# A causal-attention and LoRA layer on one core: the negated row maxima by a copy and a subtraction, and GpSimd's division one pair earlier

## The chip, the cores and the metric

The kernel runs on one core of a Trainium2 chip. The metric is the device time of one launch in microseconds (us), lower is better.

## The reference

One layer over x of shape (2, 2048, 512), float32: attention with a residual, then a feed-forward part with a residual.

```python
x = x + attn(layernorm(x), Wq, Wk, Wv, Wo)      # 16 heads of 32, rotary positions, causal
x = x + ffn(layernorm(x), base_w, base_b, router_w, router_b, lora_A, lora_B)

# attn, for each batch and head
scores = q @ k.T / sqrt(32); scores = where(causal, scores, -inf)
ctx = softmax(scores) @ v                        # then ctx @ Wo.T
# ffn: x @ base_w.T + base_b, plus 2.0 * the two best of 8 rank-16 experts
```

## The kernel before

Three stages follow one another: `project` (queries, keys and values into scratch tensors in HBM), `attend` and `finish` (output projection and feed-forward part). The change is in `attend`.

`attend` works on 8 groups, each of 4 heads of one batch entry. A group's queries are 4 tiles of 512 rows, called units, t = 0 to 3. A unit has 4(t + 1) steps, one for each block of 128 keys, 40 steps a group, and two steps make a pair: 20 pairs a group. The last pairs of the four units are 1, 5, 11 and 19.

In each step TensorE computes transposed scores of the 4 heads (`scores`, L665), ScalarE takes their exponential (L749) into a ring of 4 steps, GpSimd zeroes the later keys of a diagonal step (L605) and adds the two steps of a pair, two heads at a time (L620), and TensorE multiplies by the values (L679) and sums the pair over the keys with ones (L695, L699). GpSimd's order is `add_pairs`: for each pair the selections where they are needed, two additions of 1,024 elements a partition or fewer, and at two pairs after a unit's end the division `divide` (L630).

The exponential is of score minus row maximum. The maximum has to be there before the unit's first step, so TensorE computes the scores a second time, the other way round, in 80 items a group (`item`, L653), half a group ahead: an item is two heads by 128 queries by up to 512 keys, in one of two PSUM buffers, and item k waits until item k-2 is reduced. VectorE reduces each item (`item_max`: L769, or L775 with the causal mask for the diagonal chunk) into `part`. When the last item of a unit is reduced, `unit_max` (L781 to L797) reduces `part` over the chunks to 16 numbers a partition (4 heads by 4 blocks of queries), negates them, splits them into a part rounded to the format that the matmul reads (`F32R`) and the rest, and transposes both into `neg_rows`. SyncE's queue writes these as two more rows of the queries' stack (`shift_rows`), which two rows of ones in the keys' stack add to the scores.

The units' ends of `unit_max` fall in fixed pairs of a group: unit 2 in pair 1, unit 3 in pair 9, and unit 0 and 1 of the next group in pairs 11 and 15. The first group starts with the items of units 0 and 1 ahead of everything.

After a unit's end VectorE transposes its sums (L803), inverts them behind the next item (L807) and transposes them back behind the one after (`turn_back`, L812); GpSimd multiplies them into the unit's output (L630), which waits for L812 and for ScalarE's copy of the output; SyncE's `store` then sends it to HBM. All engines follow an order fixed in the program; VectorE's is, for each pair, the transpose of the sums if a unit ended with the pair before, then the pair's items, then `unit_max` if one is due.

Of the kernel before, what the change touches and what calls it, by code (L numbers as in the profile page):

```python
# [26 lines left out]
F32R = mybir.dt.float32r  # L27
BF16 = mybir.dt.bfloat16
ALU = mybir.AluOpType
ACT = mybir.ActivationFunctionType  # L30
AX = mybir.AxisListType

P = 128
# [7 lines left out]
SUB = TT // P  # L41
HG = 4
# [62 lines left out]
def unit_ended_before(p, pairs):  # L105

    e = p - pairs
    return [(int(e < 0), t) for t in range(QT) if LAST_PAIR[t] == e % NPAIR]


def wait_alone(eng, semaphore, value, passed):

    eng.wait_ge(semaphore, value)
    eng.sem_inc(passed, 1)
# [332 lines left out]
def attend(nc, qk_scr, v_scr, ctx_scr, shared, early):  # L447
    with ExitStack() as ctx:
        def sb(name, shape, dt=F32):
            return ctx.enter_context(nc.sbuf_tensor(name, shape, dt))  # L450

        def sem(name):
            return ctx.enter_context(nc.semaphore(name))
# [11 lines left out]
        ones = sb("a_ones", [P, DK])  # L465
        mask = sb("a_mask", [P, TT])
        part = sb("a_part", [P, HG * SUB, QT])
        max_both = sb("a_max_both", [P, 2, HG * SUB])
        neg_parts = sb("a_neg_parts", [P, 2, HG, SUB])
        neg_rows = sb("a_neg_rows", [P, 2, 32])  # L470
        st_ps = ctx.enter_context(nc.psum_tensor("a_st", [P, BANKS, TT], F32))
# [13 lines left out]
        av_copied, sum_turned = sem("a_av_copied"), sem("a_sum_turned")  # L485
        item_done, max_done = sem("a_item_done"), sem("a_max_done")
        dve_passed, pool_passed = sem("a_dve_passed"), sem("a_pool_passed")
        reduced = sem("a_reduced")
        rsum_done, rsum_turned, out_done = sem("a_rsum_done"), sem("a_rsum_turned"), sem("a_out_done")
        neg_done, rows_done = sem("a_neg_done"), sem("a_rows_done")  # L490
        ctx_stored = [sem("a_ctx_stored0"), sem("a_ctx_stored1")]
# [6 lines left out]
        def exps(g, s, h):  # L498

            return HG * NSTEP * g + HG * s + h + 1 + BANKS  # L500

        def diagonal_steps(g, s):

            t, j = STEPS[s]
            return SUB * QT * g + SUB * t + (j - t * SUB) + 1

        def pairs(g, p):

            return NPAIR * g + p + 1 + FREE
# [74 lines left out]
        @block.gpsimd  # L584
        def _(pool):
            for semaphore in (av_copied, sum_turned, out_done, rows_done, *shift_loaded, *ctx_stored):
                pool.sem_inc(semaphore, START)

            pool.memset(mask[:, :], 0.0).then_inc(zeroed, 1)
            pool.wait_ge(zeroed, 1)  # L590
            pool.affine_select(mask[:, TT - P:TT], mask[:, TT - P:TT], pattern=[[-1, P]], compare_op=ALU.is_ge,
                               fill=MASKED, base=0, channel_multiplier=1).then_inc(consts_done, 1)
            pool.wait_ge(consts_done, 1)
            for n in range(2):
                pool.memset(k_stack[n][96:98].bitcast(F32), 1.0).then_inc(key_ones, 1)
                pool.wait_ge(key_ones, n + 1)


            def drop_later_keys(g, s):

                t, j = STEPS[s]
                q0 = (j - t * SUB) * P
                block = probs[:, s % RING, :, q0:q0 + P]
                wait_alone(pool, exp_done, exps(g, s, HG - 1), pool_passed)
                pool.affine_select(block, block, pattern=[[0, HG], [1, P]], compare_op=ALU.is_ge, fill=0.0, base=0,  # L605
                                   channel_multiplier=-1).then_inc(masked, 1)

            def add_pairs(g, first):
                for p in range(NPAIR):
                    s = 2 * p  # L610
                    t, j = STEPS[s]
                    q0 = max(0, j + 1 - t * SUB) * P
                    if j >= t * SUB:
                        drop_later_keys(g, s)
                        drop_later_keys(g, s + 1)
                        pool.wait_ge(masked, diagonal_steps(g, s + 1))
                    pool.wait_ge(pair_done, pairs(g, p - 2))
                    for h in range(0, HG, 2):
                        pool.wait_ge(exp_done, exps(g, s + 1, h + 1))
                        pool.tensor_tensor(pair[:, p % 2, h:h + 2, q0:TT], probs[:, s % RING, h:h + 2, q0:TT],  # L620
                                           probs[:, (s + 1) % RING, h:h + 2, q0:TT], ALU.add).then_inc(pair_added, 1)
                    for before, t_out in unit_ended_before(p, 2):
                        if not (before and first):
                            divide(g - before, t_out)

            def divide(g, t):

                pool.wait_ge(rsum_turned, 4 * g + t + 1)
                pool.wait_ge(av_copied, 4 * g + t + 1 + START)
                pool.tensor_tensor(ctx_st[:, t % 2], ctx_st[:, t % 2], rsum_b[:, :], ALU.mult).then_inc(out_done, 1)  # L630

            add_pairs(0, True)
            with pool.Fori(1, GROUPS) as g:
                add_pairs(g, False)
            divide(GROUPS - 1, QT - 1)
# [126 lines left out]
        def _(dve):  # L762
# [18 lines left out]
            def unit_max(g, t, items):  # L781

                U = 4 * g + t
                dve.wait_ge(max_done, items + 2)
                found = part[:, :, 0:t + 1]
                dve.tensor_reduce(max_both[:, 0], found, AX.X, ALU.max, negate=True).then_inc(reduced, 1)
                dve.tensor_reduce(max_both[:, 1].bitcast(F32R), found, AX.X, ALU.max).then_inc(reduced, 1)
                dve.wait_ge(rows_done, U + START)
                dve.tensor_reduce(neg_parts[:, 0].rearrange("p h q -> p (h q)").bitcast(F32R), found, AX.X, ALU.max,
                                  negate=True).then_inc(neg_done, 1)  # L790
                dve.wait_ge(reduced, 2 * U + 2)
                with nc.allow_low_precision(reason="one exact difference, rounded as it is written"):
                    dve.tensor_reduce(neg_parts[:, 1].rearrange("p h q -> p (h q)").bitcast(F32R),
                                      max_both[:, :, :].rearrange("p n m -> p m n"), AX.X, ALU.add).then_inc(neg_done, 1)
                dve.wait_ge(neg_done, 2 * U + 2)
                dve.wait_ge(shift_loaded[t % 2], SHIFTS * (2 * g + t // 2) + START)
                dve.transpose(neg_rows[:, t % 2, :], neg_parts[:, :, :, :].rearrange("p n h q -> p (n h q)")).then_inc(rows_done, 1)  # L797

# [16 lines left out]
            def group(g, first, last):  # L815
                for p in range(NPAIR):
                    items = [(n, k) for n, k in items_of_pair(p, first) if not (n and last)]
                    ended = [(g - before, t) for before, t in unit_ended_before(p, 1) if not (before and first)]
                    for unit in ended:
                        turn_sums(*unit)  # L820
                    for i, (n, k) in enumerate(items):
                        item_max(g + n, k)
                        for unit in ended:
                            if i == 0:
                                invert(*unit)
                            if i == 1:
                                turn_back(*unit)
                    if len(items) < 2:
                        for unit in ended:
                            if not items:  # L830
                                invert(*unit)
                            turn_back(*unit)
                    for n, t in units_ended_at_pair(p, first):
                        if not (n and last):
                            issued = items_before(p + 1, first)
                            unit_max(g + n, t, NITEM * g + (min(issued, NITEM) if last else issued))
# [451 lines left out]
def layer(nc, x, wq_t, wk_t, wv_t, wo_t, rope, base_t, base_b, router_t, router_b, lora_a, lora_b, out):  # L1288

    qk_scr = nc.dram_tensor("qk_scratch", [4, GROUPS, P, SEQ], F32, kind="Internal").ap()  # L1290
    v_scr = nc.dram_tensor("v_scratch", [GROUPS, SEQ, P], F32, kind="Internal").ap()
    ctx_scr = nc.dram_tensor("ctx_scratch", [GROUPS, P, SEQ], F32, kind="Internal").ap()
    with ExitStack() as ctx:

        shared = ctx.enter_context(nc.sbuf_tensor("shared", [P, W_RING * DM], F32))[:, :]
        early = Early(nc, ctx, shared, ctx_scr, wo_t)
        project(nc, x, wq_t, wk_t, wv_t, rope, qk_scr, v_scr, shared)
        attend(nc, qk_scr, v_scr, ctx_scr, shared, early.loads)
        finish(nc, early, x, wo_t, base_t, base_b, router_t, router_b, lora_a, lora_b, out)
# [43 lines left out]
```

## Time and profile before

| | |
|---|---|
| median of 3 runs | 1798.36 us (1798.25 to 1802.1) |
| the profiled execution, its own time | 1798.25 us |
| its span, first to last instruction | 1796.3 us |
| TensorE (PE) busy | 1667.7 us, 93% |
| VectorE (DVE) busy | 1130.8 us, 63% |
| ScalarE (ACT) busy | 823.7 us, 46% |
| GpSimd (POOL) busy | 882.0 us, 49% |
| mean granted TensorE clock | 0.968 |
| the attention stage | from about 317 to 1489 us of the span |

The share of busy time is a mean over stages with different limits. A matmul's end is modelled, so a busy PE isn't a PE at its peak. Idle time of an engine costs something only where another comes to wait for it.

### The profile page before, as it was taken

What the parts mean: (1) busy time and instruction counts of PE and PEld (TensorE: products, weight loads), DVE (VectorE), ACT (ScalarE), POOL (GpSimd) and SP (SyncE); (2) the same over time, 40 slices, a digit from 0 to 9 for tenths busy, and PEclk for the clock granted to TensorE, in tenths of its full rate; (3) what the DMA queues carried; (4) which work ended last, traced back from release to release, by engine and by line L of the source; (5) the groups of instructions that cost most, each with busy time, mean ns of one, the idle gap of its engine ahead of it and who ended that gap; (6) DMA issues with size and microseconds to landing.
All of it is one profiled execution on the core that took longest, in us unless ns stands there. A gap on an engine that the chain in (4) does not pass through costs nothing. (4 is left out here: it accounts for less than half of the span.)

```text
span 1796.3 us, 30755 instructions
## 1 busy us (share of the span) xinstructions
PE 1667.7 (93%) x9440; PEld 989.6 (55%) x9440; DVE 1130.8 (63%) x2278; ACT 823.7 (46%) x1544; POOL 882.0 (49%) x558
## 2 busy tenths in 40 slices
PE   6999997599999999989999999999999985999998
PEld 5888885244454454444444444445445423777776
DVE  6667663567676676667667766767767405555664
ACT  3222221045665665646556655656656663222321
POOL 1332333346666666756667666666666672111111
PEclk9999999579999999999999999999999997999999
DMA  5556545751142133134115106107102003222321
GB/s 176 205 184 233 191 158 186 165 112 30 25 97 70 26 85 81 25 71 96 25 34 127 31 19 142 25 7 159 25 7 78 7 6 118 73 92 70 102 85 47
DMA packets 103185, 156.90 MB, mean 87 GB/s; under 512 B 10544, under 2 KB 43824, under 8 KB 100400
## 3 DMA queue, kind: packets, MB, share of 16 engines
q1 hardware_dynamic: 93296, 136.10, 28.1%
q10 hardware_dynamic: 9792, 19.40, 2.9%
q8 instruction: 74, 1.21, 0.3%
q14 instruction: 23, 0.19, 0.0%
HBM read 96.23 MB, written 58.72 MB: 86 GB/s over the span
## 5 line engine op out<-in xcount | busy, mean ns | idle before, releaser
L749 ACT ACTIVATE a_probs<-a_st 128x512 f32<-128x512 f32 (+3 forms) x1280 | 648.4, 532 | 459.3 <-PE a_st L665 416.9
L620 POOL TENSOR_TENSOR a_pair<-a_probs 128x1024 f32<-128x1024 f32 (+2 forms) x320 | 613.9, 1938 | 267.9 <-ACT a_probs L749 254.4
L769 DVE TENSOR_REDUCE a_part<-a_mx 128x2 f32<-128x1024 f32 x384 | 460.9, 1219 | 226.8 <-PE a_mx L653 226.0
L665 PE MATMUL a_st<-a_q_stack,a_k_stack 98*128 98x512 f32 (+3 forms) x1280 | 523.8, 421 | 30.2 <-ACT a_probs L749 20.6
L665 PEld LDWEIGHTS a_st<-a_q_stack,a_k_stack 98*128 98x128 f32 x1280 | 240.9, 189 | 389.2 <-ACT a_probs L749 250.0
L653 PE MATMUL a_mx<-a_k_stack,a_q_stack 96*128 96x512 f32 (+3 forms) x1280 | 380.9, 384 | 50.3 <-DMA a_q_stack<-qk_scratch 24.5
L775 DVE CUSTOM_DVE_ANT_0 a_mx<-a_mx,a_mask 128x384 f32<-128x384 f32 (+3 forms) x512 | 239.5, 515 | 100.1 <-PE a_mx L653 99.3
L653 PEld LDWEIGHTS a_mx<-a_k_stack,a_q_stack 96*128 96x128 f32 x1280 | 235.2, 197 | 106.2 <-DVE a_part L769 40.3
L211 POOL TENSOR_TENSOR p_rot<-p_mul 128x1024 f32<-128x1024 f32 x32 | 90.8, 2838 | 213.3 <-DVE p_mul L406 213.3
L605 POOL TENSOR_SCALAR_AFFINE_SELECT a_probs<-a_probs 128x512 f32<-128x512 f32 x128 | 80.9, 634 | 154.4 <-ACT a_probs L749 154.2
L985 POOL TENSOR_TENSOR f_x<-f_x,f_bias 128x512 f32<-128x512 f32 x32 | 41.3, 1324 | 230.4 <-DVE f_xn L1178 230.4
L679 PE MATMUL a_av<-a_probs,shared 128*32 128x512 f32 (+3 forms) x1280 | 151.5, 546 | 0.0
L679 PE MATMUL a_av<-a_probs,a_v 128*32 128x512 f32 (+3 forms) x1280 | 151.5, 546 | 0.0
L699 PE MATMUL a_sum<-a_pair,a_ones 128*32 128x512 f32 (+2 forms) x1280 | 140.0, 509 | 0.3 <-POOL a_pair L620 0.3
L405 DVE TENSOR_TENSOR p_mul<-p_pair,p_tab 128x1024 f32<-128x1024 f32 x32 | 39.1, 1222 | 64.4 <-PE p_pair L275 64.4
L324 ACT ACTIVATE p_rot_hi<-p_rot 128x1024 fp32r<-128x1024 f32 x32 | 34.0, 1062 | 89.3 <-POOL p_rot L211 89.3
L275 PE MATMUL p_pair<-p_xt_hi,p_w_hi 128*128 128x512 f32 x256 | 72.6, 406 | 1.6 <-DVE p_xt_lo L396 1.6
L699 PEld LDWEIGHTS a_sum<-a_pair,a_ones 128*32 128x32 f32 x1280 | 40.3, 110 | 58.1 <-issue 57.5
L775 DVE DVE_READ_ACCUMULATOR2_ANT a_part<- 128x1 f32 x512 | 72.1, 141 | 0.0
L410 DVE TENSOR_TENSOR p_rot_lo<-p_rot,p_rot_hi 128x1024 fp32r<-128x1024 f32 x32 | 50.8, 1588 | 33.1 <-ACT p_rot_hi L324 33.1
L275 PE MATMUL p_pair<-p_xt_hi,p_w_lo 128*128 128x512 f32 x256 | 70.9, 399 | 0.0
L275 PE MATMUL p_pair<-p_xt_lo,p_w_hi 128*128 128x512 f32 x256 | 70.9, 399 | 0.0
(134 smaller groups left out, 1586.4 us busy)
## 6 DMA issues: line engine op xcount, KB each, us to landing
a_q_stack<-qk_scratch SPq DMA_DIRECT2D x96, 256.0 KB, 5.1
a_k_stack<-qk_scratch SPq DMA_DIRECT2D x21, 1024.0 KB, 12.8
qk_scratch<-p_rot_hi SPq DMA_DIRECT2D x32, 512.0 KB, 3.1
qk_scratch<-p_rot_lo SPq DMA_DIRECT2D x32, 512.0 KB, 3.9
v_scratch<-p_v_st SPq DMA_DIRECT2D x32, 256.0 KB, 6.1
ctx_scratch<-a_ctx_st SPq DMA_DIRECT2D x32, 256.0 KB, 2.6
f_ctx<-ctx_scratch SPq DMA_DIRECT2D x8, 1024.0 KB, 8.8
f_x<-in_x SPq DMA_DIRECT2D x8, 1024.0 KB, 8.0
```

What stands on the lines that cost most here:

```text
L211: pool.tensor_tensor(rot[:, par], mul[:, par, :, 0, :], mul[:, par, :, 1, :], ALU.add).then_inc(rot_done, 1)
L275: mm = pe.matmul(pair_ps[p % 2][:, half, :], w[:, kt, cols], a[:, u, kt, :], start=(n == 0), stop=(n == len(passes) - 1))
L410: dve.tensor_tensor(rot_lo[:, p % 2], rot[:, p % 2], rot_hi[:, p % 2].bitcast(F32), ALU.subtract).then_inc(rot_lo_done, 1)
L605: pool.affine_select(block, block, pattern=[[0, HG], [1, P]], compare_op=ALU.is_ge, fill=0.0, base=0, channel_multiplier=-1).then_inc(mask ...
L620: pool.tensor_tensor(pair[:, p % 2, h:h + 2, q0:TT], probs[:, s % RING, h:h + 2, q0:TT], probs[:, (s + 1) % RING, h:h + 2, q0:TT], ALU.add ...
L653: mm = pe.matmul(mx_ps[k % 2][:, n, 0:width], q_stack[0:96, t, h, qi * P:(qi + 1) * P], k_stack[par][0:96, h, c * TT:c * TT + width], star ...
L665: pe.matmul(st_ps[:, n % BANKS, q0:TT], k_stack[par][0:98, h, j * P:(j + 1) * P], q_stack[0:98, t, h, q0:TT], start=True, stop=True).then_ ...
L679: mm = pe.matmul(av_ps[h * DK:(h + 1) * DK, q0:TT], vb[par][:, j, h * DK:(h + 1) * DK], probs[:, s % RING, h, q0:TT], start=j == 0, stop=s ...
L699: mm = pe.matmul(sum_ps[h * DK:(h + 1) * DK, q1:TT], ones[:, :], pair[:, p % 2, h, q1:TT], start=unit_first and q1 == q0, stop=unit_last, ...
L749: act.activation(probs[:, s % RING, h, q0:TT], st_ps[:, (HG * s + h) % BANKS, q0:TT], ACT.Exp, scale=SCORE_SCALE).then_inc(exp_done, 1)
L769: dve.tensor_reduce(heads_part[:, 2 * hp:2 * hp + 2, qi, c], mx_ps[k % 2][:, :, :], AX.X, ALU.max).then_inc(max_done, 1)
L775: ins = dve.tensor_tensor_reduce(out=mx_ps[k % 2][:, n, 0:width], in0=mx_ps[k % 2][:, n, 0:width], in1=mask[:, TT - width:TT], scale=1.0, ...
```

## The change

In `unit_max` the 16 maxima are taken and negated once, into `neg_max`; a copy rounds them into the first half of `neg_parts`, and a subtraction writes the rest into the second half. Before, four reductions made the same two halves: one negated and one rounded into `max_both`, one negated and rounded into `neg_parts`, and a sum over the pair in `max_both`. In `add_pairs` the division of a finished unit stands one pair after its end, not two. SyncE's `store` keeps its place, two pairs after.

```diff
-        max_both = sb("a_max_both", [P, 2, HG * SUB])
+        neg_max = sb("a_neg_max", [P, HG * SUB])
...
-        reduced = sem("a_reduced")
+        reduced, rounded = sem("a_reduced"), sem("a_rounded")
...
-                    for before, t_out in unit_ended_before(p, 2):
+                    for before, t_out in unit_ended_before(p, 1):
                         if not (before and first):
                             divide(g - before, t_out)
...
                 dve.wait_ge(max_done, items + 2)
-                found = part[:, :, 0:t + 1]
-                dve.tensor_reduce(max_both[:, 0], found, AX.X, ALU.max, negate=True).then_inc(reduced, 1)
-                dve.tensor_reduce(max_both[:, 1].bitcast(F32R), found, AX.X, ALU.max).then_inc(reduced, 1)
+                dve.tensor_reduce(neg_max[:, :], part[:, :, 0:t + 1], AX.X, ALU.max, negate=True).then_inc(reduced, 1)
+                dve.wait_ge(reduced, U + 1)
                 dve.wait_ge(rows_done, U + START)
-                dve.tensor_reduce(neg_parts[:, 0].rearrange("p h q -> p (h q)").bitcast(F32R), found, AX.X, ALU.max,
-                                  negate=True).then_inc(neg_done, 1)
-                dve.wait_ge(reduced, 2 * U + 2)
-                with nc.allow_low_precision(reason="one exact difference, rounded as it is written"):
-                    dve.tensor_reduce(neg_parts[:, 1].rearrange("p h q -> p (h q)").bitcast(F32R),
-                                      max_both[:, :, :].rearrange("p n m -> p m n"), AX.X, ALU.add).then_inc(neg_done, 1)
-                dve.wait_ge(neg_done, 2 * U + 2)
+                neg = neg_max[:, :].rearrange("p (h q) -> p h q", q=SUB)
+                dve.tensor_copy(neg_parts[:, 0].bitcast(F32R), neg).then_inc(rounded, 1)
+                dve.wait_ge(rounded, U + 1)
+                dve.tensor_tensor(neg_parts[:, 1].bitcast(F32R), neg, neg_parts[:, 0], ALU.subtract).then_inc(neg_done, 1)
+                dve.wait_ge(neg_done, U + 1)
```

## Rows read from the trace of the kernel before

**Rows 1.** Busy us by engine (instructions) in the steady attention stretch, clock, DMA.
```profile
core 0: us, PE busy (x) PEld busy (x) DVE busy (x) ACT busy (x) POOL busy (x), PEclk, DMA share, GB/s
400.00:1427.00 1027.00, 991.20 (x6350) 494.21 (x6349) 708.61 (x1527) 610.99 (x1203) 671.54 (x440) 1.00 0.25 56
```

**Rows 2.** Waits of PE, 400 to 1427 us: total us, times, longest.
```profile
PE a_mx L653 <- DVE a_part L769: 13.6, 34, 0.7
```

**Rows 3.** Timeline at unit 2's end: start, us, engine, line, operation, [idle before].
```profile
943.77 1.22 POOL L605 TENSOR_SCALAR_AFFINE_SELECT a_probs<-a_probs 128x512 f32<-128x512 f32 x2
...
947.61 0.64 PE L679 MATMUL a_av<-a_probs,shared 128*32 128x256 f32 x8
...
950.11 4.72 POOL L620 TENSOR_TENSOR a_pair<-a_probs 128x1024 f32<-128x1024 f32 x2 [2.19 <-ACT a_probs L749]
...
950.46 0.20 DVE L786 TENSOR_REDUCE a_max_both<-a_part 128x16 f32<-128x48 f32 x1
...
951.15 0.21 DVE L797 STREAM_TRANSPOSE a_neg_rows<-a_neg_parts 128x32 f32<-128x32 f32 x1 [0.15 <-DVE a_neg_parts L793]
...
953.62 1.17 DVE L769 TENSOR_REDUCE a_part<-a_mx 128x2 f32<-128x1024 f32 x1
...
954.70 0.70 DVE L812 STREAM_TRANSPOSE a_rsum_b<-a_rsum 128x512 f32<-128x512 f32 x1
...
955.43 0.62 PE L653 MATMUL a_mx<-a_k_stack,a_q_stack 96*128 96x512 f32 x2
...
956.33 4.71 POOL L620 TENSOR_TENSOR a_pair<-a_probs 128x1024 f32<-128x1024 f32 x2 [1.50 <-ACT a_probs L749]
```

**Rows 4.** Timeline of the projection stage: VectorE's subtraction and GpSimd's addition.
```profile
145.49 2.39 POOL L211 TENSOR_TENSOR p_rot<-p_mul 128x1024 f32<-128x1024 f32 x1 [0.80 <-DVE p_mul L406]
...
145.93 3.04 DVE L410 TENSOR_TENSOR p_rot_lo<-p_rot,p_rot_hi 128x1024 fp32r<-128x1024 f32 x1 [0.60 <-ACT p_rot_hi L324]
...
154.48 1.21 DVE L410 TENSOR_TENSOR p_rot_lo<-p_rot,p_rot_hi 128x1024 fp32r<-128x1024 f32 x1
...
154.72 3.23 POOL L211 TENSOR_TENSOR p_rot<-p_mul 128x1024 f32<-128x1024 f32 x1 [6.84 <-DVE p_mul L406]
```

**Rows 5.** Timeline of the last stage: two of GpSimd's four successive additions, one subtraction.
```profile
1518.58 1.26 POOL L985 TENSOR_TENSOR f_x<-f_x,f_bias 128x512 f32<-128x512 f32 x1
...
1519.34 1.06 DVE L140 TENSOR_TENSOR f_base_lo<-shared,f_base_hi 128x512 fp32r<-128x512 f32 x1
...
1519.81 1.72 POOL L985 TENSOR_TENSOR f_x<-f_x,f_bias 128x512 f32<-128x512 f32 x1
```

**Rows 6.** Groups by line and form: busy us, mean ns of one, idle before.
```profile
L1222 DVE COPY f_gate_x<-f_h 128x512 f32<-128x512 f32 x8 | 3.4, 427 | 0.3
```

**Rows 7.** Timeline at unit 0's end.
```profile
1018.55 4.70 POOL L620 TENSOR_TENSOR a_pair<-a_probs 128x1024 f32<-128x1024 f32 x2 [3.61 <-ACT a_probs L749]
...
1019.54 0.21 DVE L797 STREAM_TRANSPOSE a_neg_rows<-a_neg_parts 128x32 f32<-128x32 f32 x1 [0.16 <-DVE a_neg_parts L793]
...
1021.25 1.20 DVE L769 TENSOR_REDUCE a_part<-a_mx 128x2 f32<-128x1024 f32 x1
...
1023.66 0.63 PE L653 MATMUL a_mx<-a_k_stack,a_q_stack 96*128 96x512 f32 x2
```

**Rows 8.** Timeline at unit 1's end.
```profile
910.45 4.72 POOL L620 TENSOR_TENSOR a_pair<-a_probs 128x1024 f32<-128x1024 f32 x2 [3.65 <-ACT a_probs L749]
...
913.72 2.36 DVE L769 TENSOR_REDUCE a_part<-a_mx 128x2 f32<-128x1024 f32 x2 [1.53 <-PE a_mx L653]
...
915.00 0.44 PE L653 MATMUL a_mx<-a_k_stack,a_q_stack 96*128 96x128 f32 x2 [0.40 <-DVE a_part L769]
```

**Rows 9.** Timeline at unit 3's end.
```profile
1007.06 0.64 POOL L605 TENSOR_SCALAR_AFFINE_SELECT a_probs<-a_probs 128x512 f32<-128x512 f32 x1 [2.03 <-ACT a_probs L749]
...
1008.96 0.43 DVE L775 CUSTOM_DVE_ANT_0 a_mx<-a_mx,a_mask 128x256 f32<-128x256 f32 x1 [1.58 <-PE a_mx L653]
```

**Rows 10.** Timeline of PE near the kernel's end.
```profile
1780.60 0.69 PE L1054 MATMUL f_out_ps<-f_b_hi,f_mt_hi 128*128 128x512 f32 x1 [2.17 <-DVE f_mt_lo L1231]
```

**Rows 11.** Busy us by engine and clock (the third number from the end) behind it.
```profile
1780.60:1786.00 5.40, 5.40 (x17) 4.23 (x18) 1.38 (x2) 0.00 (x0) 0.00 (x0) 0.68 0.00 2
```

## Prediction

> **What bounds the kernel now.** The change lies in the attention stage, so I read the busy time by stretch first. In [rows 1] TensorE is busy for 991.2 of 1027 us, at its full clock, while VectorE has 709 and GpSimd 672. Whatever holds TensorE back here is paid in full, and a delay on VectorE or GpSimd is paid only where TensorE comes to wait for it. The list of waits, second, says how near that is: TensorE already waits for the running maxima of VectorE, 34 times in this stretch and never over 0.7 us [rows 2]. The two `a_mx` buffers give VectorE little room: item k may be multiplied only when item k-2 has been reduced. Third I read the timeline around each place that the change touches, for how much room is left there.
>
> **What VectorE does at a unit's end, before.** The chain is three reductions that don't depend on each other, a fourth that does, and the transpose. In [rows 3] it runs from 950.46 to 951.36 (951.15 + 0.21), 0.90 us, for the unit t = 2. GpSimd's pair addition runs all that time (950.11 to 954.83, two instructions of about 2.36) and the chain isn't slowed by it.
>
> **What it does after.** One reduction, a copy that needs it, a subtraction that needs both, the transpose. Three dependent steps instead of two. A step behind two waits starts 0.16 us after its predecessor's end, as the transpose does [rows 3], so with about 0.2 us for each small instruction the free-running chain takes 0.2 + 0.16 + 0.2 + 0.03 to 0.16 + 0.2 + 0.16 + 0.21, about 1.1 to 1.3 us: 0.2 to 0.4 longer than before, times 32 units. If that were all it would cost nearly nothing, since VectorE is idle for 1.5 us after most of these places; only in the first 30 us, where TensorE waits on VectorE item by item, would 0.3 us show.
>
> **The term that decides: GpSimd.** The projection stage shows what an instruction of VectorE with two inputs in SBUF does beside a GpSimd addition. Alone, the subtraction of line 410 takes 1.21 us; started at 145.93 inside an addition that ends at 147.88, it takes 3.04, that is, it ends 1.09 us after the addition [rows 4]. It was held for all the rest of it. The other way round, an addition started at 154.72 inside such a subtraction takes 3.23 instead of 2.39. So the two exclude one another for whole instructions. The last stage shows who comes next when additions stand back to back: GpSimd's second, 1518.58 to 1519.84, holds the subtraction of 1519.34 (1.06 us); then the subtraction goes, and it is the third addition, nominally begun at 1519.81, that is stretched to 1.72 us [rows 5]. VectorE slips in between two additions.
> The reductions of before, and the maxima in PSUM with the mask, show none of this beside GpSimd (the chain of [rows 3] runs inside an addition). The new subtraction has two SBUF inputs, `neg_max` and `neg_parts[:, 0]`. The new copy has one; no row shows such a copy beside GpSimd. One row bears on it: a copy of 512 elements in SBUF takes 427 ns [rows 6], while the subtraction of 1024 takes 1.21 us, so the copy moves more than one element in a cycle, and I take it to use the same second path. Bounds: it is never held (0), or held to the end of the addition under way. I take the upper one.
> The Trainium skill (SBUF — State Buffer, Who interferes with whom) says that reductions never contend with GpSimd, that a copy does when it runs in the two-port mode, and that a `tensor_tensor` with both inputs in SBUF contends with GpSimd's reads, the later one being blocked wholly. By that rule the sum is the one below; without its sentence on copies it would be the smaller one of the first rival.
>
> **Priced place by place.** Each unit's chain falls at a fixed place in the loop of 20 pairs, four places in a group.
> Unit t = 2 [rows 3]. The copy is due at 950.46 + 0.19 + 0.16 = 950.81, the first addition ends at 952.47; the copy goes then, till 952.6. The second addition follows and holds the subtraction till 954.95; that is done at 955.1, the transpose runs from 955.25 to 955.46, 4.1 us late. Behind it VectorE has the transpose of the sums and an item, and begins the next item, k = 50, 2.10 us later (951.36 to 953.62, less 0.16 of waiting): 957.56, done 1.17 later at 958.73. TensorE's item k = 52 needs that; it began at 955.43 and now begins at 958.78. Loss 3.35 us.
> Unit t = 0 [rows 7]. The additions run from 1018.55 to 1023.25. By the same steps the transpose ends at 1023.86 instead of 1019.75. The item of 1021.25 began 1.50 after that end, so it now runs from 1025.36 to 1026.56, and TensorE's item of 1023.66 begins at 1026.61. Loss 2.95 us.
> Unit t = 1 [rows 8]. Additions till 915.17, the transpose ends at 915.86. VectorE's item of 913.72 begins at 915.95 and ends at 917.1, and TensorE's item that now starts at 915.00, already 0.40 late, starts at 917.15. Loss 2.15 us.
> Unit t = 3 [rows 9]. Only a selection of 0.64 us is near (1007.06), and VectorE's next item is 1.58 us of idle away. At worst 0.64 + 0.4 later: nothing lost.
> The places repeat with the same offsets in all groups: seven each for the first three, since the first group is filled from a head start. Sum 7 x (3.35 + 2.95 + 2.15) = 59.2. The first group's own t = 2, beside a shorter addition, and the start: about 1.5, an estimate. Together 61 us.
>
> **The clock.** TensorE would now stand still for 2 to 2.7 us at 21 places. Before the end of the kernel it stood for 2.17 us and then ran at 0.68 of its clock over 5.4 us, that is partly at the lower of its two levels, 1.2 GHz: 1.7 us lost [rows 10, 11]. Bounds for 21 places: 0 and 36 us. I put in 5, a seventh, as most gaps have work close on both sides.
>
> **The earlier division.** GpSimd's division (1.28 us) goes from behind the second pair after a unit's end to behind the first. Costs and gains: after unit 3 it stands ahead of the selections of 943.77, which end at 946.3 instead of 945.0, and TensorE wants the first at 947.61: hidden, 1.9 us to spare for the selection it needs first. After unit 0, it waits for the transposed reciprocals (954.70 + 0.70) after the additions' end at 954.83, and the next addition begins 0.35 later than 956.33, with 3 us in hand before its sums. Even with VectorE 4 us late, the division ends at 960.7, where that next addition could begin at 959.7 and is wanted at 968. Nothing frees a buffer that anyone waits for: the store stays where it is in SP's queue. 0 us, with bounds of -0.5 and +1 a group. SP's other issues, the shift rows among them, are due several pairs before they are used.
>
> **Sum.** Span 1796.3 + 61 + 5 = 1862; its own time is 1.95 us above the span (1798.25), which is the median of the runs to 0.1. 1864 us.
>
> **Rivals.**
> - *One hold instead of two* (the copy isn't held). The subtraction alone, due at 951.0, waits till 952.45; the transpose ends at 952.96, 1.6 late; TensorE loses 1.0 at t = 2 and 0.5 at t = 0, nothing at t = 1. 7 x 1.5 + 1 = 11 us: 1810. For it: no row shows a held copy. Against: [rows 6].
> - *No hold for so small an instruction*, the other side. Instructions of 16 elements might pass between GpSimd's accesses; the held ones of [rows 4, 5] have 512 and 1024. Then three small instructions replace four, the chain is about as long, and the time is 1798 to 1800, no change. It decides if a copy or subtraction in a running addition takes under 0.3 us. The skill (VectorE: DVE Perf Modes, Rules for kernel authors) advises to minimise the count of chained instructions, which by itself would make this part a gain, at most 32 x 0.1 us on an engine with time to spare.
> - *The clock falls nearly each time*: 61 + 36, 1895. For it: [rows 10, 11]. Against: 2.17 us is the shortest gap that I found a fall behind, and most of the new ones would be about that or broken up by short work.
> - *Faster*: the division's move removes a wait that the trace doesn't name. Nothing speaks for it; 2 us at best.
>
> **Chances.** Two holds 0.66; one hold 0.13; no hold 0.12; two holds and the low clock 0.05; faster 0.04. The two-hold case alone spans 1845 to 1885 (the places' sum off by a quarter, clock 0 to 15). To leave out no more than two in ten the range must reach the one-hold case: 1806 to 1890. A measurement here can tell about 0.2%, 3.6 us, from no change: faster 0.04, same 0.12, slower 0.84.
>
> **What would show it.** In the changed trace the copy or the subtraction of a unit's end should last 1.5 to 2.4 us at three of four places and under 0.3 at the fourth; the transpose should end about 4 us after the reduction; TensorE's waits for `a_part` should grow from 0.7 to 2 to 3 us, three in each group, and each group should be 8 to 9 us longer. Divisions should begin one pair earlier with no wait of TensorE behind them. Small instructions at 0.2 us beside additions prove the prediction wrong; so does a group of unchanged length.

## The result, and the profile after

The change makes the kernel slower: 1892.78 us median of 4 runs (1881.79 to 1897.07) against 1798.68 us (1798.25 to 1802.1, 4 runs), a ratio of 1.051 with a 95% interval of 1.0462 to 1.0556. That is 94 us more, 29 us above the forecast of 1864 and 3 us above the top of the range. The profiled execution took 1886.59 us, its span is 1884.6 us, 88.3 us longer than before, and its mean granted clock is 0.945, before 0.968.

The chain first. The rows of its three last instructions give the least, median and longest duration in ns, then the first and last start in us:

```profile
L789 DVE CAST a_neg_parts<-a_neg_max x32: 174/1218/1929, 337.4 to 1513.5; 128x16 fp32r<-128x16 f32 x32
L791 DVE TENSOR_TENSOR a_neg_parts<-a_neg_max,a_neg_parts x32: 174/2291/2320, 337.6 to 1513.7; 128x16 fp32r<-128x16 f32 x32
L794 DVE STREAM_TRANSPOSE a_neg_rows<-a_neg_parts x32: 211/211/214, 337.8 to 1514.2; 128x32 f32<-128x32 f32 x32
```

The copy (shown as CAST) and the subtraction move 16 elements a partition and take 174 ns when nothing is in the way; half of the copies take 1.2 us or more, half of the subtractions 2.3 us or more. The timeline at a unit 2's end shows why; it answers to [rows 3]:

```profile
995.02 4.71 POOL L620 TENSOR_TENSOR a_pair<-a_probs 128x1024 f32<-128x1024 f32 x2 [2.18 <-ACT a_probs L749]
995.37 0.20 DVE L785 TENSOR_REDUCE a_neg_max<-a_part 128x16 f32<-128x48 f32 x1
...
995.70 1.73 DVE L789 CAST a_neg_parts<-a_neg_max 128x16 fp32r<-128x16 f32 x1
...
997.47 2.30 DVE L791 TENSOR_TENSOR a_neg_parts<-a_neg_max,a_neg_parts 128x16 fp32r<-128x16 f32 x1
...
999.94 0.21 DVE L794 STREAM_TRANSPOSE a_neg_rows<-a_neg_parts 128x32 f32<-128x32 f32 x1 [0.17 <-DVE a_neg_parts L791]
...
1001.94 0.44 PE L653 MATMUL a_mx<-a_k_stack,a_q_stack 96*128 96x128 f32 x2 [1.90 <-DVE a_part L769]
...
1003.18 1.22 PE L653 MATMUL a_mx<-a_k_stack,a_q_stack 96*128 96x512 f32 x2 [0.52 <-DVE a_part L769]
...
1003.90 1.28 POOL L630 TENSOR_TENSOR a_ctx_st<-a_ctx_st,a_rsum_b 128x512 f32<-128x512 f32 x1 [4.16 <-DVE a_rsum_b L809]
```

GpSimd's two additions run from 995.02 to 999.73, the first to about 997.4. The copy ends at 997.43, with the first; the subtraction, which needs the copy, gets no room between the two and ends at 999.77, with the second. From the start of the reduction to the end of the transpose it is 4.78 us, before 0.90. TensorE, which waited 0.7 us at most in [rows 2], now waits 1.90 and then 0.52 us.

At a unit 0's end the same holds stand (copy 1.74, subtraction 2.29), and the wait ends with VectorE's L775:

```profile
1075.50 0.44 PE L653 MATMUL a_mx<-a_k_stack,a_q_stack 96*128 96x128 f32 x2 [1.50 <-DVE a_part L775]
...
1076.69 0.73 PE L653 MATMUL a_mx<-a_k_stack,a_q_stack 96*128 96x512 f32 x2 [0.46 <-DVE a_part L769]
```

At a unit 3's end no addition is under way, and the chain runs free, 1.11 us from 1057.10 to 1058.21:

```profile
1057.10 0.22 DVE L785 TENSOR_REDUCE a_neg_max<-a_part 128x16 f32<-128x64 f32 x1
1057.45 0.17 DVE L789 CAST a_neg_parts<-a_neg_max 128x16 fp32r<-128x16 f32 x1
1057.66 0.17 DVE L791 TENSOR_TENSOR a_neg_parts<-a_neg_max,a_neg_parts 128x16 fp32r<-128x16 f32 x1
1058.00 0.21 DVE L794 STREAM_TRANSPOSE a_neg_rows<-a_neg_parts 128x32 f32<-128x32 f32 x1 [0.17 <-DVE a_neg_parts L791]
```

TensorE's waits for the maxima over the whole span (total us, times, longest). Before, these two rows had 21.2 us in 47 times and 4.1 us in 12:

```profile
PE a_mx L653 <- DVE a_part L769: 53.6, 68, 2.2
...
PE a_mx L653 <- DVE a_part L775: 13.8, 18, 1.5
```

That is 42 us more waiting, less than half of the 88. The rest is in the clock, as the experiments with repeated matmuls will show. The stretch that answers to [rows 1], and five stretches of 2 us behind the wait of unit 2 above (the granted clock is the third number from the end):

```profile
400.00:1513.00 1113.00, 1035.44 (x6321) 507.07 (x6324) 774.99 (x1489) 612.03 (x1200) 668.77 (x437) 0.95 0.23 52
1000.00:1002.00 2.00, 0.10 (x2) 0.06 (x1) 2.00 (x5) 0.60 (x1) 0.00 (x0) 1.00 1.11 226
1002.00:1004.00 2.00, 1.48 (x5) 1.07 (x6) 2.00 (x6) 0.60 (x1) 0.10 (x1) 0.74 1.22 298
1004.00:1006.00 2.00, 2.00 (x7) 0.64 (x10) 1.45 (x3) 1.09 (x2) 2.00 (x2) 0.50 1.08 209
1006.00:1008.00 2.00, 2.00 (x16) 0.40 (x8) 0.00 (x0) 0.00 (x0) 2.00 (x2) 0.50 1.06 232
1008.00:1010.00 2.00, 2.00 (x7) 1.02 (x4) 0.00 (x0) 0.41 (x1) 1.81 (x1) 0.56 0.66 218
```

Full speed while TensorE waits, then half of it, the 1.2 GHz level, for some 7 us, nearly six of them without a gap in TensorE's work. The mean of [rows 1] was 1.00, and 0.95 is the mean here. By the trace's record of the granted clock it falls behind 19 of the 21 late places (seven each at the ends of units 2, 0 and 1), and stays low for 3.4 to 10.2 us each time, 102 us in all.

Both kernels issue the same 9,440 matmuls in the same order, so one can be laid on the other. In the steady part the lag grows at three places of each group alone, those of units 2, 0 and 1, and not at unit 3's. Over the seven units 2 it grows by 34.0 us, over the seven units 0 by 29.3, over the seven units 1 by 28.2, 91.5 in all; 3 us are won back elsewhere, over 2 of them in the first group, where the low clock at the stage's start ends at 371.5 us and not at 377.9. It does so in some runs and not in others: with the division alone it ended at 370.8, with the chain alone at 378.2.

### The profile page after: what moved, and what is told of

It reads as the page before. It is cut to its first block and busy times, and to the rows that moved or that the text cites. A ratio compares the mean times of both kernels' runs of the same rounds, so it can differ in the third digit from the quotient of the medians.

```text
span 1884.6 us, 30755 instructions
## 1 busy us (share of the span) xinstructions
PE 1713.1 (91%) x9440; PEld 1001.3 (53%) x9440; DVE 1201.0 (64%) x2246; ACT 826.3 (44%) x1544; POOL 881.6 (47%) x558
## 5 line engine op out<-in xcount | busy, mean ns | idle before, releaser
L769 DVE TENSOR_REDUCE a_part<-a_mx 128x2 f32<-128x1024 f32 x384 | 460.9, 1218 | 234.2 <-PE a_mx L653 233.2
L665 PE MATMUL a_st<-a_q_stack,a_k_stack 98*128 98x512 f32 (+3 forms) x1280 | 531.1, 429 | 29.7 <-ACT a_probs L749 20.3
L653 PE MATMUL a_mx<-a_k_stack,a_q_stack 96*128 96x512 f32 (+3 forms) x1280 | 392.3, 393 | 93.1 <-DVE a_part L769 53.6
L665 PEld LDWEIGHTS a_st<-a_q_stack,a_k_stack 98*128 98x128 f32 x1280 | 247.2, 194 | 395.0 <-ACT a_probs L749 239.8
L775 DVE CUSTOM_DVE_ANT_0 a_mx<-a_mx,a_mask 128x384 f32<-128x384 f32 (+3 forms) x512 | 239.0, 513 | 108.3 <-PE a_mx L653 108.3
L679 PE MATMUL a_av<-a_probs,shared 128*32 128x512 f32 (+3 forms) x1280 | 161.7, 579 | 0.0
L679 PE MATMUL a_av<-a_probs,a_v 128*32 128x512 f32 (+3 forms) x1280 | 157.1, 565 | 0.0
L699 PE MATMUL a_sum<-a_pair,a_ones 128*32 128x512 f32 (+2 forms) x1280 | 148.7, 538 | 0.3 <-POOL a_pair L620 0.3
L630 POOL TENSOR_TENSOR a_ctx_st<-a_ctx_st,a_rsum_b 128x512 f32<-128x512 f32 x32 | 40.9, 1279 | 69.2 <-DVE a_rsum_b L809 69.2
L775 DVE DVE_READ_ACCUMULATOR2_ANT a_part<- 128x1 f32 x512 | 72.2, 141 | 0.0
```

The source lines that it names most:

```text
L653: mm = pe.matmul(mx_ps[k % 2][:, n, 0:width], q_stack[0:96, t, h, qi * P:(qi + 1) * P], k_stack[par][0:96, h, c * TT:c * TT + width], star ...
L665: pe.matmul(st_ps[:, n % BANKS, q0:TT], k_stack[par][0:98, h, j * P:(j + 1) * P], q_stack[0:98, t, h, q0:TT], start=True, stop=True).then_ ...
L679: mm = pe.matmul(av_ps[h * DK:(h + 1) * DK, q0:TT], vb[par][:, j, h * DK:(h + 1) * DK], probs[:, s % RING, h, q0:TT], start=j == 0, stop=s ...
L699: mm = pe.matmul(sum_ps[h * DK:(h + 1) * DK, q1:TT], ones[:, :], pair[:, p % 2, h, q1:TT], start=unit_first and q1 == q0, stop=unit_last, ...
L769: dve.tensor_reduce(heads_part[:, 2 * hp:2 * hp + 2, qi, c], mx_ps[k % 2][:, :, :], AX.X, ALU.max).then_inc(max_done, 1)
L775: ins = dve.tensor_tensor_reduce(out=mx_ps[k % 2][:, n, 0:width], in0=mx_ps[k % 2][:, n, 0:width], in1=mask[:, TT - width:TT], scale=1.0, ...
```

## The experiments

**The division alone.**

```diff
-                    for before, t_out in unit_ended_before(p, 2):
+                    for before, t_out in unit_ended_before(p, 1):
```

> The kernel before with the division alone moved one pair ahead. Theory (the chain does all the harm): GpSimd's selections and additions behind the division move by at most 1.3 us and TensorE never waits for them, so 1798 to 1800 us, ratio 0.999 to 1.002. Rival (the division does part of the harm, since GpSimd then waits for VectorE ahead of its next additions): some us a group, 1810 or more.

Measured: 1798.3 us (1796.35 to 1804.73, 12 runs), ratio 0.9988 (0.9974 to 1.0002). In the timeline the division now stands ahead of the next pair's additions, which begin 1.98 us after the last ones' end instead of 1.50, and nobody comes to wait for them:

```profile
949.16 2.38 POOL L620 TENSOR_TENSOR a_pair<-a_probs 128x1024 f32<-128x1024 f32 x1
952.28 1.29 POOL L630 TENSOR_TENSOR a_ctx_st<-a_ctx_st,a_rsum_b 128x512 f32<-128x512 f32 x1 [0.74 <-DVE a_rsum_b L812]
953.52 4.71 POOL L620 TENSOR_TENSOR a_pair<-a_probs 128x1024 f32<-128x1024 f32 x2
```

The division costs nothing, as forecast.

**The chain alone**: the changed kernel with the division back behind the second pair.

```diff
-                    for before, t_out in unit_ended_before(p, 1):
+                    for before, t_out in unit_ended_before(p, 2):
```

> The changed chain, with the division back at two pairs. Theory: the copy lasts 1.2 to 1.8 us and the subtraction 2.3 us at three of four places as in the changed kernel, time 1880 to 1897 us. Rival (division): clearly below the changed kernel, by the 10 us or more that the moved division adds when VectorE is late.

Measured: 1894.19 us (1891.17 to 1895.73, 4 runs), ratio 1.0513 (1.0487 to 1.054), TensorE's wait on L769 53.2 us in 67 times, clock 0.941. The whole loss is the chain's.

**Only the subtraction.** The rounded half comes from a second reduction, as it did before, and the subtraction stays. The chain then has one instruction that GpSimd could hold.

```diff
                 dve.tensor_reduce(neg_max[:, :], part[:, :, 0:t + 1], AX.X, ALU.max, negate=True).then_inc(reduced, 1)
-                dve.wait_ge(reduced, U + 1)
                 dve.wait_ge(rows_done, U + START)
-                dve.tensor_copy(neg_parts[:, 0].bitcast(F32R), neg).then_inc(rounded, 1)
+                dve.tensor_reduce(neg_parts[:, 0].rearrange("p h q -> p (h q)").bitcast(F32R), part[:, :, 0:t + 1],
+                                  AX.X, ALU.max, negate=True).then_inc(rounded, 1)
+                dve.wait_ge(reduced, U + 1)
                 dve.wait_ge(rounded, U + 1)
```

> The changed chain, but the rounded half comes from a second reduction and not from the copy; the subtraction with two SBUF inputs stays, the division is at two pairs. Theory (each of the two is held for what is left of the addition under way): one hold of 1.4 to 1.9 us for the subtraction, the transpose ends 1.6 us later than before, TensorE loses 1.0 us at the end of unit 2, 0.5 at unit 0 and nothing at unit 1, and gaps this short leave the clock up: 1806 to 1815 us. Rival (a hold lasts to the end of both additions, whichever instruction asks): the subtraction lasts over 4 us and the time stays at 1880 or more.

Measured: 1801.62 us (1799.66 to 1804.58, 10 runs), ratio 1.001 (0.9996 to 1.0023). The timeline at a unit 2's end:

```profile
947.99 4.71 POOL L620 TENSOR_TENSOR a_pair<-a_probs 128x1024 f32<-128x1024 f32 x2 [2.19 <-ACT a_probs L749]
948.34 0.20 DVE L785 TENSOR_REDUCE a_neg_max<-a_part 128x16 f32<-128x48 f32 x1
...
948.46 0.20 DVE L788 TENSOR_REDUCE a_neg_parts<-a_part 128x16 fp32r<-128x48 f32 x1
...
948.69 1.72 DVE L792 TENSOR_TENSOR a_neg_parts<-a_neg_max,a_neg_parts 128x16 fp32r<-128x16 f32 x1
...
950.57 0.21 DVE L795 STREAM_TRANSPOSE a_neg_rows<-a_neg_parts 128x32 f32<-128x32 f32 x1 [0.17 <-DVE a_neg_parts L792]
```

Both reductions pass inside the addition in 0.20 us each, and the subtraction is held to the end of the first one. The hold is as forecast. Its price isn't: the transpose is 1.54 us late (2.44 from the reduction's start, before 0.90), and TensorE loses 0.3 us at unit 2 and nothing at unit 0, where the expectation had 1.0 and 0.5; the time lies below its 1806 to 1815 us, and can't be told from no change.

**Only the copy.** Before's chain, with the third reduction replaced by a copy of the first one's output.

```diff
-                dve.tensor_reduce(neg_parts[:, 0].rearrange("p h q -> p (h q)").bitcast(F32R), found, AX.X, ALU.max,
-                                  negate=True).then_inc(neg_done, 1)
                 dve.wait_ge(reduced, 2 * U + 2)
+                dve.wait_ge(rows_done, U + START)
+                dve.tensor_copy(neg_parts[:, 0].bitcast(F32R),
+                                max_both[:, 0].rearrange("p (h q) -> p h q", q=SUB)).then_inc(neg_done, 1)
```

> The chain of before, but the rounded half is copied from the unrounded one and not reduced again; no subtraction. Theory (a copy of 16 elements takes GpSimd's path too): the copy lasts 1.4 to 1.9 us beside an addition, the sum behind it 0.2 us, time 1806 to 1815 us. Rival (the copy is slow only because it is the instruction ahead of a held subtraction): under 0.3 us and 1799 us.

Measured: 1804.14 us (1801.88 to 1810.08, 10 runs), ratio 1.0027 (1.0012 to 1.0043). The copy and the reduction behind it, in ns:

```profile
L790 DVE CAST a_neg_parts<-a_max_both x32: 174/1123/1831, 336.6 to 1428.2; 128x16 fp32r<-128x16 f32 x32
L793 DVE TENSOR_REDUCE a_neg_parts<-a_max_both x32: 172/174/181, 336.7 to 1428.7; 128x16 fp32r<-128x32 f32 x32
```

A copy of 16 elements is held too, to 1.83 us; a reduction of 32 never is. At a unit 2's end the transpose is 1.62 us late and TensorE loses 0.4 us, at a unit 0's 0.1; the time is again below the 1806 to 1815 us expected. By their ratios the two edits apart cost 2 and 5 us (0.001 and 0.0027 of 1798, the first with an interval that holds 1); summed over the places in the traces it is 2.1 and 3.6 us. Together they cost 94.

**The waits filled.** In the changed kernel the scores' matmul just ahead of each of the 21 late items, and of the same item in the first group, where nothing is late, is issued six more times, with the same operands and output, so that TensorE works where it waited. It tells the clock's share from the waiting itself.

```diff
-            def scores(g, par, s, h):
+            def scores(g, par, s, h, extra=0):
...
-                pe.matmul(st_ps[:, n % BANKS, q0:TT], k_stack[par][0:98, h, j * P:(j + 1) * P],
-                          q_stack[0:98, t, h, q0:TT], start=True, stop=True).then_inc(st_done, 1)
+                for _ in range(extra + 1):
+                    mm = pe.matmul(st_ps[:, n % BANKS, q0:TT], k_stack[par][0:98, h, j * P:(j + 1) * P],
+                                   q_stack[0:98, t, h, q0:TT], start=True, stop=True)
+                mm.then_inc(st_done, 1)
...
+                            extra = 6 if i < len(due) and due[i] == late else 0
```

> The changed kernel, with one scores matmul repeated six more times (about 0.2 us each, same result, written over itself) right ahead of each of the 21 items for which TensorE waits longest: the gap is mostly filled with work that nobody needs. Theory (some 49 us of the loss are waits, some 40 the lower clock behind them): the waits' ends don't move, the granted clock stays at 1.0 there, and the time falls to 1845 to 1865 us although TensorE does more. Rival (all of the loss is waiting, the clock's fall costs nothing since VectorE sets the pace): 1882 to 1897 us as without the repeats, or more.

Measured: 1853.92 us (1849.44 to 1856.65, 4 runs), ratio 1.0303 (1.0266 to 1.034). With 132 more matmuls (22 places) it is 39 us faster than the changed kernel. Holds, waits and clock:

```profile
L793 DVE CAST a_neg_parts<-a_neg_max x32: 174/1221/1929, 336.9 to 1478.4; 128x16 fp32r<-128x16 f32 x32
L795 DVE TENSOR_TENSOR a_neg_parts<-a_neg_max,a_neg_parts x32: 174/2290/2325, 337.1 to 1478.6; 128x16 fp32r<-128x16 f32 x32
```

```profile
PE a_mx L653 <- DVE a_part L773: 34.3, 67, 1.3
```

```profile
400.00:1478.00 1078.00, 1029.15 (x6451) 516.86 (x6455) 773.09 (x1490) 611.77 (x1199) 669.20 (x437) 0.99 0.23 54
```

VectorE is held exactly as in the changed kernel and the items are late as there; TensorE's idle time is shorter, and the clock no longer falls at the ends of units 0 and 1. At those of unit 2 it still falls, six times of seven, for 3.4 us, though the waits ahead are only two of 0.51 us:

```profile
983.92 0.73 PE L653 MATMUL a_mx<-a_k_stack,a_q_stack 96*128 96x512 f32 x2 [0.52 <-DVE a_part L773]
```

```profile
986.00:988.00 2.00, 2.00 (x12) 0.22 (x4) 0.05 (x1) 0.01 (x1) 2.00 (x1) 0.50 1.01 207
```

The mean of 0.99 hides these six, and the expectation, a clock of 1.0 at all the places, missed them. Laid over the kernel before, a unit 0 now costs 2.2 us and a unit 1 1.8, which is about their items' lateness (2.36 and 1.76 us in the changed kernel); a unit 2 costs 4.3 us with the fall and 2.5 in the one case without. So the 39 us are what the prevented and shortened falls had cost, and not all of the clock's share. By the two ratios it is 1.051 - 1.0303, 37 us of 1798, and with both intervals (0.0047 and 0.0037, together 0.006) about 37 ± 11.

**The same repeats in the kernel before.** The edit is that of the last experiment, made to the kernel before.

> The same repeats in the kernel before, where there are no such gaps. Both theories: 21 x 6 x 0.22 = 27 us more TensorE work with nothing to hide it, 1820 to 1828 us. It gives the price of the repeats by themselves; under 1805 would mean that TensorE isn't the bound at these places.

Measured: 1821.0 us (1820.07 to 1828.81, 4 runs), ratio 1.0118 (1.0087 to 1.0149). By themselves the repeats cost 23 us, about 132 times 0.17, so they aren't a gain of their own: what they win in the changed kernel they win by standing in its waits.

**Shorter additions.** In the changed kernel GpSimd adds one head at a time, four instructions a pair instead of two.

```diff
-                    for h in range(0, HG, 2):
-                        pool.wait_ge(exp_done, exps(g, s + 1, h + 1))
-                        pool.tensor_tensor(pair[:, p % 2, h:h + 2, q0:TT], probs[:, s % RING, h:h + 2, q0:TT],
-                                           probs[:, (s + 1) % RING, h:h + 2, q0:TT], ALU.add).then_inc(pair_added, 1)
+                    for h in range(HG):
+                        pool.wait_ge(exp_done, exps(g, s + 1, h))
+                        pool.tensor_tensor(pair[:, p % 2, h, q0:TT], probs[:, s % RING, h, q0:TT],
+                                           probs[:, (s + 1) % RING, h, q0:TT], ALU.add).then_inc(pair_added, 1)
...
-                pe.wait_ge(pair_added, 2 * (NPAIR * g + p) + 2)
+                pe.wait_ge(pair_added, 4 * (NPAIR * g + p) + 4)
```

> The changed kernel, with GpSimd's additions in four instructions of one head (about 1.28 us) and not two of two heads (2.37 us). Theory (a hold lasts for the rest of one GpSimd instruction): the copy lasts 0.6 to 0.9 us, the subtraction 1.3 us, the transpose ends some 1.7 us later than before and not 3.9, TensorE's loss is 0.5 to 1.2 us a place and the clock mostly stays up: 1808 to 1825 us. Rival (holds last until GpSimd has no work): as long as in the changed kernel, 1880 us or more.

Measured: 1813.74 us (1808.74 to 1815.57, 6 runs), ratio 1.0074 (1.0048 to 1.01). The timeline at a unit 2's end:

```profile
952.96 5.00 POOL L620 TENSOR_TENSOR a_pair<-a_probs 128x512 f32<-128x512 f32 x4 [0.90 <-ACT a_probs L749]
...
954.02 0.20 DVE L785 TENSOR_REDUCE a_neg_max<-a_part 128x16 f32<-128x48 f32 x1
...
954.36 1.15 DVE L789 CAST a_neg_parts<-a_neg_max 128x16 fp32r<-128x16 f32 x1
...
955.54 1.21 DVE L791 TENSOR_TENSOR a_neg_parts<-a_neg_max,a_neg_parts 128x16 fp32r<-128x16 f32 x1
...
956.92 0.21 DVE L794 STREAM_TRANSPOSE a_neg_rows<-a_neg_parts 128x32 f32<-128x32 f32 x1 [0.17 <-DVE a_neg_parts L791]
```

An addition now takes 1.25 us, and each small instruction is held for at most one of these (the copy for longer than the 0.6 to 0.9 us expected). The hold follows the length of GpSimd's instruction, and with it 79 of the 94 us are gone: the transpose is 2.21 us late instead of 3.88, TensorE loses 1.0 us at unit 2, 0.5 at unit 0 and 0.1 at unit 1, and the clock stays up at these places (mean 0.966). It falls once where before it didn't, behind two waits of 0.45 us for ScalarE near the stage's end, and 4.2 us are lost there.

**Later additions.** In the changed kernel both additions wait for all four exponentials of the pair's second step, which moves their start behind most of the chain.

```diff
-                        pool.wait_ge(exp_done, exps(g, s + 1, h + 1))
+                        pool.wait_ge(exp_done, exps(g, s + 1, HG - 1))
```

> The changed kernel with both chains as they are; GpSimd's first addition of a pair waits for the exponentials of all four heads of the second step and not of two, which starts it some 1.25 us later. Theory (the loss hangs on an addition being under way when VectorE comes to the copy): at the ends of units 2 and 0 copy and subtraction are through before the addition starts and take 0.2 us each; at unit 1 the copy is through and the subtraction is held for one addition, 2.2 us, worth 1 us to TensorE; the clock stays up. 1800 to 1812 us, over 80 us less than the changed kernel, by a wait more. Rival (the small instructions are slow by themselves or by their dependence): 1885 us or more.

Measured: 1806.95 us (1804.12 to 1825.56, 11 runs), ratio 1.005 (1.0027 to 1.0073). The same three instructions, and their timeline at a unit 2's end:

```profile
L789 DVE CAST a_neg_parts<-a_neg_max x32: 174/175/177, 337.0 to 1432.7; 128x16 fp32r<-128x16 f32 x32
L791 DVE TENSOR_TENSOR a_neg_parts<-a_neg_max,a_neg_parts x32: 174/175/2374, 337.2 to 1432.9; 128x16 fp32r<-128x16 f32 x32
```

```profile
953.87 0.18 DVE L789 CAST a_neg_parts<-a_neg_max 128x16 fp32r<-128x16 f32 x1
...
954.08 0.17 DVE L791 TENSOR_TENSOR a_neg_parts<-a_neg_max,a_neg_parts 128x16 fp32r<-128x16 f32 x1
...
954.38 4.74 POOL L620 TENSOR_TENSOR a_pair<-a_probs 128x1024 f32<-128x1024 f32 x2 [3.37 <-ACT a_probs L749]
```

The chain is word for word that of the changed kernel, and without an addition beside it it costs next to nothing. Only unit 1's subtraction still meets one (up to 2.37 us); it costs 0.7 us a group. So the loss comes from the meeting of the two engines and not from the chain's length.

None of these beats the kernel before: the nearest is the division alone, whose interval holds 1.

## Why the prediction missed its number

The direction, the two holds and the places were right. The step that failed is the size of one term, the clock: "Bounds for 21 places: 0 and 36 us. I put in 5, a seventh". It measured about 43 us. The other large term, the waits, was 12 us too large, so the total missed by less than the clock alone did; that is luck.

| term | predicted | measured |
|---|---|---|
| free chain, from its reduction's start | 1.1 to 1.3 us | 1.11 us |
| copy and subtraction at unit 2 | 1.8 and 2.35 us | 1.73 and 2.30 us |
| transpose late at unit 2 | 4.1 us | 3.88 us |
| TensorE's late item at unit 2 / 0 / 1 | 3.35 / 2.95 / 2.15 us | 2.84 / 2.36 / 1.76 us |
| unit 3 | 0 | 0 |
| lateness of the items in all | 61 us | 49 us |
| clock | 5 us | about 43 us |
| division | 0 | 0 |

*The two holds.* Confirmed, for both instructions, by the copy-only and the subtraction-only kernels, which hold each by itself, and by the two edits on GpSimd, which shorten or remove the holds with the chain unchanged. The Trainium skill (SBUF — State Buffer, Who interferes with whom) says that the engine that issues first keeps the shared ports for its whole instruction, and that reductions don't take part; the trace agrees, with 1.73 and 2.30 us for two instructions that take 0.17 alone, and 0.17 to 0.20 for the reductions beside the same additions. The Trainium skill (VectorE: DVE Perf Modes, Rules for kernel authors) advises to minimise the count of chained instructions. The runs don't bear that out here: three in place of four cost 94 us.

*The waits.* At unit 2 the late item begins 7.81 us after the reduction (995.37 to 1003.18), before 4.97, so 2.84 later; at unit 0 2.36, at unit 1 1.76. Seven times their sum is 48.7 us, 12 less than forecast; 1.5 of the 12 are the first group's, whose chains run free. For the rest, the reason shows when the runs are put side by side at unit 2: one hold makes the transpose 1.54 and 1.62 us late and costs 0.3 and 0.4, short additions 2.21 and 1.0, two holds 3.88 and 2.84. Each time it is the lateness less 1.0 to 1.3 us. The prediction's step ("done 1.17 later ... TensorE's item k = 52 needs that") left a cover of only 0.75 (4.1 less 3.35), since it kept the spacing of before, 2.10 us from the transpose's end to the next but one item of VectorE; it is 1.81 here (1000.15 to 1001.96), as VectorE, once late, finds its items ready. The rest of the 0.51 us at unit 2 is the transpose, 3.88 us late and not 4.1. The cover is also why the one-hold rival was priced too high, 1.5 us a group where 0.3 to 0.5 were lost at TensorE: one hold nearly fits into the cover, and two are far beyond it. So 2 and 5 us apart become 94 together.

*The clock.* By the laid-over traces the late places cost 91.5 us, of which 48.7 are the items' lateness; the other 43 lie in the microseconds behind them, where the same matmuls take longer, and the windows show 0.50. The seven ends of unit 1 show the price with the wait nearly constant (2.05 to 2.16 us): they cost 1.8 us twice, where the clock stayed up, 3.3 once, where it was low for 3.4 us, 4.5 twice for 6.8 us, and 6.2 twice for 10.2 us. The filled kernel takes 37 ± 11 us away by experiment and leaves six falls at some 1.7 us each; with these it is 47 ± 11, which agrees.

The forecast's reason, "most gaps have work close on both sides", is refuted: [rows 10, 11] already had a fall behind 2.17 us, and here falls stand behind 1.90 and 0.52 us with 0.7 us of work between. The trace of the kernel before had more against it, in the very stretch of [rows 1] that the prediction read as "at its full clock". Its mean of 1.00 is rounded and hides two falls, of 6.8 and 3.4 us, behind stops of TensorE in the middle of dense work ("issue": it waited for nothing that the profile shows):

```profile
799.78 0.57 PE L665 MATMUL a_st<-a_q_stack,a_k_stack 98*128 98x256 f32 x1 [3.07 <-issue]
1080.34 0.38 PE L665 MATMUL a_st<-a_q_stack,a_k_stack 98*128 98x256 f32 x1 [3.28 <-issue]
```

```profile
800.00:802.00 2.00, 2.00 (x6) 1.69 (x7) 0.76 (x1) 0.77 (x2) 1.06 (x1) 0.50 1.05 213
1081.00:1084.00 3.00, 3.00 (x14) 1.41 (x13) 2.69 (x7) 1.18 (x4) 1.00 (x2) 0.50 0.99 202
```

The upper bound, 36, was itself too low, since 21 places cost 2.0 us on average and not 1.7. The rival "the clock falls nearly each time" had 1895 and a chance of 0.05; it was the case that came true (19 of 21). That its number is only 2 us off is luck in part, as its waits were 12 us too large and its clock about 7 too small. The term deserved at least the middle of its bounds: 61 + 18 would have been 1877.

The changed kernel's runs spread by 15 us, and the clock with them: the run of 1881.79 us had a mean of 0.947, that of 1897.07 us 0.939. The profiled one, with 0.945, is among the quicker; that is why its span grew by 88 us and the median by 94.

*What stays open.* When the clock falls and when not. At unit 1's end TensorE waited 2.16 us each time, and once the clock stayed up, once it fell. The rows of TensorE and the windows behind them, first without, then with the fall:

```profile
959.90 0.44 PE L653 MATMUL a_mx<-a_k_stack,a_q_stack 96*128 96x128 f32 x2 [2.16 <-DVE a_part L769]
```

```profile
805.10 0.69 PE L653 MATMUL a_mx<-a_k_stack,a_q_stack 96*128 96x128 f32 x2 [2.16 <-DVE a_part L769]
```

```profile
960.00:961.00 1.00, 1.00 (x7) 0.46 (x11) 1.00 (x2) 0.34 (x1) 0.00 (x0) 1.00 0.05 8
...
807.00:809.00 2.00, 2.00 (x10) 0.79 (x3) 0.00 (x0) 0.05 (x1) 0.00 (x0) 0.50 0.01 2
```

The first place cost 1.8 us in all, the second 4.5. Matmuls of the same forms surround both, and in the kernel with the waits filled the clock fell behind waits of 0.51 us, so the length of the wait alone doesn't decide; what does was not tried.

## What to carry to other kernels

Before an instruction is put in for another on VectorE, ask what GpSimd is doing at that moment, and not how many elements it has: a small copy or subtraction in SBUF can cost a whole GpSimd instruction, a reduction doesn't, and two dependent ones beside successive additions cost two. A hold costs next to nothing while it fits into the slack that the pacing engine leaves (some 1.0 to 1.3 us here), and what goes beyond it is paid, so price the sum of the delays at one place, not each edit by itself. Where TensorE sets the pace, a repeated wait of about 2 us should be priced with its clock: here that nearly doubled it, and moving or cutting the other engine's work won back 79 to 86 of the 94 us.

## What was unexpected of the hardware

TensorE's clock went to its lower level after waits of 1.4 to 2.2 us between stretches of dense work, at 19 of 21 places, and stayed there for 3.4 to 10.2 us (0.74, 0.50, 0.50, 0.56 in windows of 2 us at the one shown), at a price of about 2 us a place. With six repeated matmuls in each wait it stayed up at 15 of the 21, and at the other six it fell behind two waits of 0.51 us. Waits of the same 2.16 us ended differently. And a copy of only 16 elements a partition, 0.17 us by itself, is held for what is left of GpSimd's instruction: 1.73 us beside additions of 2.36 us, 1.15 beside additions of 1.25.
